# Recurrence of a hybrid kernel: three states driven by transposes, four shared with GpSimd, the gate projected behind the convolution

## What is computed

```
xp, z  = split(x @ W_in)
xc     = silu(conv2(xp) + conv_b)
dt_r, Bc, Cc = split(xc @ W_x)
dt     = softplus(dt_r @ W_dt + b_dt)
h[s,t] = exp(dt[t] * A[s]) * h[s,t-1] + dt[t] * xc[t] * Bc[s,t]     s = 0..15
y      = sum over s of h[s] * Cc[s]  +  D * xc
out    = (y * silu(z)) @ W_out
```

## Time and profile before

| | us |
|---|---|
| median of 3 runs | 944.47 (943.37 to 945.66) |
| the profiled execution | 945.53 |
| its span, first to last instruction | 943.8 |
| DVE busy in the span | 711.9 (75%) |
| POOL busy | 549.7 (58%) |
| ACT busy | 508.9 (54%) |
| PE busy | 829.2 (88%) |

### The profile page before, as it was taken

How to read it: one execution, slowest core, us unless ns; L and a number is a source line. 1 busy time by engine, 2 the same in 40 slices (tenths; PEclk the granted TensorE clock), 3 DMA queues, 4 the chain that set the end, 5 groups by cost and what they waited for, 6 DMA issues and landing times. The chain is left out here.

```text
span 943.8 us, 10168 instructions
## 1 busy us (share of the span) xinstructions
PE 829.2 (88%) x2974; PEld 487.8 (52%) x2974; DVE 711.9 (75%) x767; ACT 508.9 (54%) x702; POOL 549.7 (58%) x373
## 2 busy tenths in 40 slices
PE   5579897979899898985587899989999999999997
PEld 1224342433333333332134554548888888888886
DVE  1999999999999999999965445655666655566655
ACT  4645666556566566643315456555555554555554
POOL 4678989999998998976736965303222121222120
PEclk9799999999999999997987999999999999999999
DMA  7959897889969898896609800001433433233433
GB/s 177 335 211 331 312 334 276 339 285 330 324 255 367 312 321 307 288 325 230 209 0 134 162 0 1 1 1 46 134 106 117 134 94 130 90 105 118 134 96 82
DMA packets 75924, 178.22 MB, mean 189 GB/s; under 512 B 24578, under 2 KB 25620, under 8 KB 75876
## 3 DMA queue, kind: packets, MB, share of 16 engines
q1 hardware_dynamic: 75892, 177.85, 57.8%
HBM read 175.57 MB, written 2.26 MB: 188 GB/s over the span
## 5 line engine op out<-in xcount | busy, mean ns | idle before, releaser
L455 POOL TENSOR_TENSOR prod<-hidden,c_wide 128x1024 f32<-128x1024 f32 x128 | 300.2, 2358 | 64.1 <-DVE hidden L888 60.4
L551 PE MATMUL ps_y<-prod,ident 128*128 128x512 f32 x512 | 242.7, 618 | 31.7 <-POOL prod L455 31.5
L888 DVE TENSOR_TENSOR_SCAN hidden<-decay,ps_d 128x1024 f32<-128x1024 f32 x92 | 209.9, 2282 | 8.3
L1923 PE MATMUL ps_conv<-hankel,u_high 128*128 128x512 f32 (+1 forms) x768 | 215.3, 361 | 0.0
L551 PEld LDWEIGHTS ps_y<-prod,ident 128*128 128x128 f32 x512 | 98.1, 197 | 172.0 <-issue 116.7
L1923 PEld LDWEIGHTS ps_conv<-hankel,u_high 128*128 128x128 f32 x768 | 138.6, 189 | 25.5 <-DVE u_t L1786 0.2
L1923 PE MATMUL ps_conv<-hankel,u_low 128*128 128x512 f32 (+1 forms) x384 | 138.1, 360 | 0.0
L2040 DVE TENSOR_TENSOR stack<-ps_conv,stack 64x512 fp32r<-64x512 f32 x128 | 88.3, 690 | 62.0 <-ACT stack L2007 59.6
L1751 POOL CAST block_mix<-even 128x256 fp32r (+1 forms) x32 | 12.7, 398 | 208.5 <-PE sums L1792 208.5
L2040 DVE TENSOR_TENSOR qk<-ps_conv,qk 64x512 fp32r<-64x512 f32 x128 | 88.3, 690 | 50.2 <-ACT qk L2007 47.5
L874 DVE TENSOR_TENSOR ps_d<-ps_x,b_wide 128x1024 f32<-128x1024 f32 x92 | 113.4, 1232 | 4.6
(11 more groups left out here) (283 smaller groups left out, 1154.5 us busy)
## 6 DMA issues: line engine op xcount, KB each, us to landing
b_wide<-bc_rows SPq DMA_DIRECT2D x128, 512.0 KB, 5.6
c_wide<-bc_rows SPq DMA_DIRECT2D x128, 512.0 KB, 5.3
hankel<-filters SPq DMA_DIRECT2D x32, 1026.0 KB, 5.2
plus<-in_M_phi_plus SPq DMA_DIRECT2D x2, 1024.0 KB, 12.8
minus<-in_M_phi_minus SPq DMA_DIRECT2D x2, 1024.0 KB, 18.0
x_pair<-in_x SPq DMA_DIRECT2D x2, 768.0 KB, 8.2
bc_rows<-mixed_and_low SPq DMA_DIRECT2D x8, 128.0 KB, 4.7
out<-plus SPq DMA_DIRECT2D x8, 128.0 KB, 3.6
```

Of the source, the lines that this page charges most:

```text
L455: nc.gpsimd.tensor_tensor(prod[k % PAIR][:, :], hidden[k % DEEP][:, :], c_wide[s % BC_DEEP][:, :], ALU.mult).then_inc(prod_ready, 1)
L551: mm = nc.tensor.matmul(out, ident[:, :], halves(prod[k % PAIR])[h], start=False, stop=(k % N == N - 1))
L888: nc.vector.tensor_tensor_scan(hidden[k % DEEP][:, order], left[:, order], right[:, order], 0.0, ALU.mult, ALU.add).then_inc(hidden_ready, 1)
L1923: mm = nc.tensor.matmul(out, pairs[q][wp][:, 2 * delta + source, :], rows, start=(delta == 0 and term == 0), stop=(delta == 2 * half + 1 a ...
```

## The change

States 2, 7, 10 and 15 are now POOL's, the first three with their decay in `ps_w`. States 3, 8 and 11 are *turned*: their drive is made with time on the partitions. PE transposes dt * xc and the rows of B once per unit into `ps_w` (`turn_late`, `turn_early`), ACT takes them out (`take_turned`); for each turned state ACT multiplies eight 128x128 blocks by a column of B as the activation's scale (`scale_drive`), and PE transposes them back into `ps_d` (`turn_drive`) while DVE scans the state before. Nine drives of a unit stay with DVE, where there were eleven; in unit 7, where state 7 is turned and 2 and 6 are shared, thirteen where there were fifteen. z is projected after the convolution has been taken out of `ps_w`, and silu is applied to it straight from there. The gate product follows the scan of state 2. D * xc is an ACT copy with a scale into `ps_y`. The relu stays in `ps_w` in place of an addition by PE. xc has one tile in place of two.

```
-POOL_STATES = (2, 3, 6, 9, 15)
-WIDE_SHARED = POOL_STATES[1:4]
+POOL_STATES = (2, 7, 10, 15)
+TURNED_STATES = (3, 8, 11)
+WIDE_SHARED = POOL_STATES[0:3]
...
-        LAST_SHARE = POOL_STATES[2:3]
+        LAST_SHARE = (2, 6)
+        LAST_TURNED = (7,)
...
                 def gate_in(u, i, b):
-                    pe.wait_ge(dtx_ready, u)
+                    pe.wait_ge(xc_ready, u + 1)
                     project(i, b, w_gate[i], z_ready)
...
+                def turn_drive(u, s, last=False):
+                    scanned(u, s - 2)
+                    for half in range(2):
+                        pe.wait_ge(drive_t_ready, 2 * turned_before(u, s, last) + half + 1)
+                        for t in range(half * SPANS, (half + 1) * SPANS):
+                            mm = nc.tensor.transpose(ps_d[:, t * 128:(t + 1) * 128], drive_t[:, t, :], ident[:, :])
+                    mm.then_inc(drive_turned, 1)
...
                             if s == Y_LAG:
+                                if s in turned(not ahead):
+                                    turn_drive(u, s, not ahead)
                                 if i == 0 and not first:
                                     out_product(b - 1)
                                     conv_in(v, j, bv)
-                                    pe.wait_ge(g.mixed_ready, b)
-                                skip_in(u, i)
...
-                                sum_states(n - Y_LAG, (k - Y_LAG) % (2 * N))
+                                sum_states(n - Y_LAG, (k - Y_LAG) % (2 * N), u if s == Y_LAG else None)
+                            if s > Y_LAG and s + 1 in turned(not ahead):
+                                turn_drive(u, s + 1, not ahead)
+                            if s == 0:
+                                turn_early(u)
...
+                                    conv_in(v, j, bv)
+                                if s == Y_LAG + (i == 1 or first):
                                     gate_in(v, j, bv)
...
+                def skip_in(u, i, taken=0):
+                    at_least(act, gated_ready, u)
+                    at_least(act, g.mixed_ready, taken)
+                    nc.scalar.activation(ps_y[:, :], xc[:, :], ACT.Copy, scale=cols[i][:, 1:2]).then_inc(skip_ready, 1)
...
+                def scale_drive(u, s, last=False):
+                    act.wait_ge(dtx_t_ready, 3 * u + 3)
+                    at_least(act, drive_turned, turned_before(u, s, last))
+                    for t in range(TILES):
+                        part = nc.scalar.activation(drive_t[:, t, :], dtx_t[:, t, :], ACT.Copy, scale=b_t[:, t, s:s + 1])
+                        if t % SPANS == SPANS - 1:
+                            part.then_inc(drive_t_ready, 1)
...
+                                if s == 2:
+                                    shared_decay_of(u, i, LAST_SHARE[0], hidden_ready, u * N + LAST_SHARE[0], final)
                                 if s == 3:
+                                    skip_in(u, i)
...
+                            if s == 0:
+                                shared_decay_of(u, i, WIDE_SHARED[0], dtx_t_ready, 3 * u + 3)
+                                scale_drive(u, 3)
+                            if s == 1:
+                                decay_of(u, i, 3)
+                                decay_of(u, i, 4)
                             if s == 2:
-                                take_z(v, j, first=first and i == 0)
-                                shared_decay_of(u, i, POOL_STATES[0], hidden_ready, u * N + POOL_STATES[0])
-                                shared_decay_of(u, i, WIDE_SHARED[0], z_taken, v)
-                            if s == 3:
+                                decay_of(u, i, 5)
...
+                                if first or i == 1:
+                                    skip_in(u, i)
+                                else:
+                                    norm_take(b - 1)
+                                    skip_in(u, i, taken=b)
+                                if not first and i == 1:
+                                    norm_silu(nc, act, g, b - 1)
+                                silu_input(v, j)
                                 silu_gate(v, j)
...
                                 nc.scalar.preload_act_table_set("natural_log_exp_and_others")
                             if s == 4:
-                                shared_decay_of(u, i, WIDE_SHARED[1], xc_ready, v + 1)
-                            if s == 6 and i == 0 and not first:
-                                norm_squares(nc, act, g, b - 1, rectified[0:C, :], mixed[:, :])
+                                decay_of(u, i, 6)
+                                shared_decay_of(u, i, WIDE_SHARED[1], gate_ready, v + 1)
+                            if s == 6:
+                                scale_drive(u, 8)
+                                decay_of(u, i, 8)
+                                if i == 0 and not first:
+                                    norm_squares(nc, act, g, b - 1, soft[0:C, :], mixed[:, :])
                             if s == 7:
+                                decay_of(u, i, 9)
                                 take_low(v, j)
                                 shared_decay_of(u, i, WIDE_SHARED[2], dt_low_ready, v + 1)
+                                scale_drive(u, 11)
...
+                            if s == 14:
+                                decay_of(v, j, 0, last and i == 0)
                             if s == N - 1:
-                                shared_decay_of(u, i, POOL_STATES[4], hidden_ready, u * N + POOL_STATES[4])
+                                shared_decay_of(u, i, POOL_STATES[3], hidden_ready, u * N + POOL_STATES[3])
                                 keep_dtx(v)
                                 decay_of(v, j, 1, last and i == 0)
+                                take_turned(v)
...
-                            if s == 1 and not (first and i == 0):
+                            if s == 2 and not (first and i == 0):
                                 gate_of(u - 1, 1 - i, b)
```

More of the change, by code:

```diff
@@ L297, in mamba_stage, with wide, turned, decayed_before @@
         AHEAD = 2
-        LAST_SHARE = POOL_STATES[2:3]
+        LAST_SHARE = (2, 6)
+        LAST_TURNED = (7,)
         def shared(last):
             return LAST_SHARE if last else POOL_STATES
+        def wide(last):
+            return LAST_SHARE[1:] if last else WIDE_SHARED
+        def turned(last):
+            return LAST_TURNED if last else TURNED_STATES
         def driven_before(u, s, last=False):
+            return (N - SHARE - TURNED) * u + s - sum(p < s for p in shared(last) + turned(last))
+        def decayed_before(u, s, last=False):
             return (N - SHARE) * u + s - sum(p < s for p in shared(last))
@@ L307, in shared_before, with turned_before, spread_order, b_slot @@
             return SHARE * u + sum(p < s for p in shared(last))
+        def turned_before(u, s, last=False):
+            return TURNED * u + sum(p < s for p in turned(last))
+        def spread_order(last):
+            return [(i, s) for i in range(2) for s in range(N) if s not in turned(last and i == 1)]
+        SLOT_ORDER = (0, 1, 2, 3) * 2 + (0, 1, 2) + (0, 1, 2, 3) * 3 + (0, 1, 2)
+        def b_slot(i, s, last):
+            at = spread_order(last).index((i, s))
+            return SLOT_ORDER[at] if at < len(SLOT_ORDER) else at - len(SLOT_ORDER)
+        def b_loads(b, i, s, last):
+            slot = b_slot(i, s, last)
+            rank = sum(b_slot(j, p, last) == slot for j, p in spread_order(last) if (j, p) < (i, s))
+            return 16 * (b * SLOT_ORDER.count(slot) + rank + 1)
         def own_states(last):
@@ L383, in unit @@
                     for s in range(N):
-                        spread_b(u, i, s)
+                        if s not in turned(u == 2 * B - 1):
+                            spread_b(u, i, s)
                         if u or s:
@@ L553, in sum_states @@
+                def sum_states(n, k, seeded=None):
+                    pe.wait_ge(prod_ready, n + 1)
+                    if seeded is not None:
+                        pe.wait_ge(skip_ready, seeded + 1)
+                    for h, out in enumerate(halves(ps_y)):
+                        mm = nc.tensor.matmul(out, ident[:, :], halves(prod[k % PAIR])[h], start=False, stop=True,
+                                              skip_group_check=True)
                     mm.then_inc(prod_summed, 1)
@@ L735, in decay_of, with shared_decay_of @@
                                          scale=a_neg[i][:, s:s + 1]).then_inc(decay_ready, 1)
-                def shared_decay_of(u, i, s, taken, count):
+                def shared_decay_of(u, i, s, taken, count, final=False):
                     act.wait_ge(taken, count)
-                    nc.scalar.activation((ps_w if s in WIDE_SHARED else ps_d)[:, :], dt[i][:, :], ACT.Exp,
+                    nc.scalar.activation((ps_w if s in wide(final) else ps_d)[:, :], dt[i][:, :], ACT.Exp,
```

(15 more changed lines are left out.)

180 lines of the change are left out of this document (90 added, 90 removed).

## The result

The changed kernel takes 978.02 us (median of 4 runs, 975.81 to 978.49) beside 945.07 for the kernel before on the same chip (943.37 to 949.09): ratio 1.0338, 95% interval 1.0301 to 1.0374. That is 33 us slower; forecast were 11, with 968 as the upper end. The direction was right, the size was not, and the range missed. The profiled execution took 977.91, its span is 976.1.

The account below looks back on a forecast made before the run. DVE was taken to bound the kernel, POOL close behind. Terms -21.4 + 17.5 + 9.0 + 2.4 + 1.1 + 2.5 = +11.1 us on the profiled 945.53 gave 956.6, or 955.6 against the median; range 943 to 968, some 8 in 10.

Parts of the forecast that it names:

- The gain: DVE over all units: 16 drives removed at 1.34 us each, 21.4 us saved, at least 19.7.
- The first rival: Scan 6: DVE never waits there and B[10] lands in time, so the drives' saving goes through; 929 us, chance 0.14.
- The chain to decay 6: ACT and PE, gate product to state 6's decay: scan 6 waits in units 1 to 6, 17.5 us (11.8 to 21.1).
- the choice of 4.2, 2.1 and 1.4: Waits in us taken before scan 6: 4.2 in units 2, 4, 6; 2.1 in unit 1; 1.4 in units 3, 5.
- B[10] behind the squares: SP's load, units 2, 4, 6: held until ACT has squared, POOL's drive late, scan 10 waits 3.0 us each, 9.0 together.
- The second rival: Scan 10: B[10] is covered, only the wait before scan 6 remains, 9.0 us fall away; 946.6 us, chance 0.12.
- the first cost: Waits before scan 6 in units 1 to 6 for state 6's late decay on ACT: 17.5 us, bounds 11.8 and 21.1.
- The third cost: Scan 15, units 1 to 6: waits for dt's taking, then decays 0 and 15; 0.4 us each, 2.4 together, bounds 0 and 6.
- dt's projection ... starts about 1.0 after scan 10: PE behind POOL's drive 10 and product 8: projection starts 1.0 us after scan 10, dt taken 11 us later.
- The last unit: Unit 7: 1.2 us before scan 2 for decay 2, and `norm_x` waiting 1.34 more for POOL; 2.5 us.
- the **first: Unit 0: wait of 1.19 before scan 2 goes, turned drive 3 0.6 late, decay 6 some 1.7; 1.1 us net.
- the third rival: ACT's two table switches before decay 6 each drain one activation, units 1 to 6: 13.6 us more, 969 us, chance 0.08.

Follow-up runs that it names:

- run with held clock: Changed kernel with the eight transposes of state 3's drive issued three times over the same tile, values unchanged; 959.86 us, ratio to the kernel before 1.0177.
- the first experiment: Changed kernel with the gate product back behind the scan of state 1 instead of state 2; 956.75 us, ratio to the kernel before 1.0129.
- third experiment: Changed kernel with the next unit's decay 0 behind decay 15 and the kept product in ACT's list; 970.30 us, ratio to the kernel before 1.0263.

## Why the prediction was right in direction and wrong in size

- **The gain** was right: 16 drives, 20.7 us of DVE's busy time. The first rival (the gain goes through) fell with the scans of state 6, which wait in every unit from 0 to 6.
- **The chain to decay 6** was right in every link; at full clock it gives the waits of the run with held clock, 12.8 against 11.8 at the low end. The step that failed is the choice of 4.2, 2.1 and 1.4 for half clock. In the even units the chain of unit 4's rows gave 4.7 (its link to the end of ACT's taking adds up to 6.6, not 6.5), and I took 4.2, between that and full clock; it was 5.25 to 5.88. In the odd units I added at most 1.5, from one group of four instructions. I called them two additions' worth; but four instructions are one addition ("x4" of line 607), so by my own row the addition and the convolution, eight instructions, would have cost twice as much. After the change PE idles 3.37 there, not 2.40, and in unit 5 both the addition (3.75) and the convolution (3.19) ran at the lower level, 3.1 more than with the clock held (1.96 and 1.88); the waits are 3.2 to 3.6. I had carried over the penalty of one instruction group, not of all that runs until the clock is back. Cost of the step: 8.9.
- **B[10] behind the squares** was right, place and price: 8.4 against 9.0. The second rival (only the first cost) fell with it; the run with the store moved shows the mechanism alone.
- **The third cost, scan 15,** is where most of the miss lies, 12.0. The step that failed is "dt's projection ... starts about 1.0 after scan 10". I had named the reason myself, drive 10 ahead of product 8 in POOL's list, and then not followed it: product 8 takes its 2.36 after drive 10 (302.14), its addition follows at 304.54, 3.27 long because PE had idled 2.71 and its clock fell, and dt's projection starts at 307.75, 5.5 after scan 10. From there to the taking of dt it took 11.25, where 11 were forecast. That makes the waits at scan 14 (1.4 to 1.5) and dt (0.5) in the even units, 5.8 in all where I had none. Most of it is the clock again: in unit 4 of the first experiment, with the same order and the addition in 1.98, dt's projection starts 4.2 after scan 10, and scan 14 doesn't wait. Scan 15 waits 1.0 in all six units, the upper bound of the sum, where I took 0.4 (3.7 more): decay 0 and decay 15 (1.15 and 1.10) together are longer than the product of dt beside them (1.23). The waits before scan 11 in the odd units, 0.7 to 1.0 (2.5 in all), I had not seen: decay 11 stands behind the low-rank copy, a decay and eight scalings.
- **The last unit** was right, 2.5. In the **first** I was 1.6 short: decay 6 was 3.37 late there, where 1.7 were forecast.
- **The table loads** don't drain, so the third rival fell. D * xc ends at 281.13, the load stands at 281.23 and lasts 1.28, the silu follows at 282.52. The drain of 1.38 of the Trainium skill, page "ScalarE: Activation LUTs", section "What ACT_TABLE_LOAD costs", is not in these rows, after the change as before.
- **The range** ended at 968 because two of its bounds were too low: 21.1 and 6 for the first and third cost, where 26.4 and 14.4 came (the second kept within its 11.7). Both hold PE's lower clock, which I had priced in the one by unit 4's rows and one group of four instructions, and not at all in the other. And each term stood by itself, while B[10]'s delay fed two: POOL's drive is late for scan 10, product 8 behind it is late too, PE idles, its clock falls, and dt is late.

## What to carry to other kernels

When an engine that bounds a kernel loses work, list for each step that now falls due earlier what stands ahead of it in the in-order lists of the engines that feed it, and follow the delay past the first wait until someone has slack. Here four moves of whole instructions in those lists, with no work removed, turned 33 us lost into 11 won, and with two more it was 14. If a delay leaves PE idle, take as a bound that everything PE does next runs at the lower clock, until a row shows it back at the higher one.

## What was not expected of the hardware

- Extra work made the kernel faster: 24 transposes in place of 8 ahead of the gate product (2.84 us instead of 1.09) kept the granted clock at 1.00 where it had been 0.59 and 0.55, and took 18 us off the whole. With eight transposes and the output product right behind them the clock stayed at 1.00 too (first experiment, 262 to 268), so there the missing pause was enough. Whether the extra work or the shorter pause (0.38 instead of 2.13) held it with 24 was not told apart. That transposes alone can raise it, unit 0 of the same run shows: from 26.52 on PE ran nothing else, and in its 24 (33.26 to 38.04) the granted clock was 0.50 from 34 to 36, 0.67 from 36 to 38 and 1.00 from 38 to 40.
- The lower level lasted unequally long, behind pauses of the same length too. In the kernel before, each behind a pause of 2.40 or 2.41 us, D * xc and the addition after it took 3.02 and 2.59 in unit 1, 1.98 and 1.88 in unit 3, 3.51 and 2.10 in unit 5. Behind product 8 a pause of 2.27 brought the lower level (third experiment, unit 4) and one of 2.36 did not (first experiment, unit 4). So one row of the kernel before could not give the price, and what decides it stays open.
- Eight scalings of 128x128 took 2.43 us on ACT. Each is 0.39 long, where the plain copy of the earlier trace rows is 0.30, but one follows another after 0.29, so they overlap.
